# A two-layer macaron block on one core: the second feed-forward's first group moved into the slot attention's last two rounds, and the order at two other stage changes rewritten

## What is computed

```python
x = x + 0.5 * moe(ln(x))        # 8 experts, top 2, hidden = relu(x w1)^2
x = x + linear_attention(ln(x))
x = x + 0.5 * moe(ln(x))
x = x + 0.5 * ffn(ln(x))        # below
x = x + slot_attention(ln(x))   # 16 heads, softmax over the 8 batches of a position
x = x + 0.5 * ffn(ln(x))

def fp4_linear(x, w):           # both operands put on the FP4 grid in blocks of 16
    return fp4_quant_dequant(x) @ fp4_quant_dequant(w).T
h = silu(fp4_linear(x, w_gate)) * fp4_linear(x, w_up)   # 128 -> 352
y = fp4_linear(h, w_down)                               # 352 -> 128
```

## Time and profile before

| | us |
|---|---|
| median of 3 runs | 785.92 (783.46 to 788.07) |
| the profiled execution | 783.95 |
| its span, first to last instruction | 782.2 |
| busy: PE / DVE / ACT / POOL | 674.8 (86%) / 612.6 (78%) / 455.9 (58%) / 277.0 (35%) |
| mean granted TensorE clock | 0.95 |
| chain of waits: PE / DVE / ACT | 62% / 18% / 12% |

### The profile page before, as it was taken

How to read it: one execution, slowest core, us unless ns; L and a number is a source line. 1 busy time by engine, 2 the same in 40 slices (tenths; PEclk the granted TensorE clock), 3 DMA queues, 4 the chain that set the end, 5 groups by cost and what they waited for, 6 DMA issues and landing times.

```text
span 782.2 us, 16363 instructions
## 1 busy us (share of the span) xinstructions
PE 674.8 (86%) x5826; PEld 481.0 (61%) x5826; DVE 612.6 (78%) x1566; ACT 455.9 (58%) x863; POOL 277.0 (35%) x405
## 2 busy tenths in 40 slices
PE   4999999699999699999976999588888882799985
PEld 2777767568878667777743656355645651365654
DVE  2788778656675687788788999587999985699984
ACT  3777788647556067777864766356454215366752
POOL 5001120264554201001105686331543452367620
PEclk9999999789999899999998999889999996799998
DMA  8000000000000000000000000000000000000000
GB/s 208 12 0 0 0 1 1 2 3 4 2 0 4 2 1 1 0 0 0 1 2 0 1 0 1 1 0 1 2 0 0 0 1 0 0 14 28 13 28 28
DMA packets 13460, 7.08 MB, mean 9 GB/s; under 512 B 1176, under 2 KB 13408, under 8 KB 13408
## 3 DMA queue, kind: packets, MB, share of 16 engines
q1 hardware_dynamic: 11328, 5.33, 2.6%
q10 hardware_dynamic: 2080, 1.05, 0.5%
HBM read 4.28 MB, written 2.10 MB: 8 GB/s over the span
## 4 chain that ended last, share of the span: by engine, by line
PE 62%; DVE 18%; ACT 12%; issue 5%; POOL 2%; DMA 1%; DVEq 0%; ACTq 0%; POOLq 0%
PE ps L1390 57%; DVE shared L1226 3%; DVE shared L1198 3%; ACT ffn_work L509 2%; PE ps L1739 2%; ACT ffn_work L777 2%; PE ps L1398 1%; ACT xn L547 1%; DVE x_sb L1027 1%; ACT x_sb L785 1%; ACT ffn_work L770 1%; ACT xnT L554 1%; DVE stats L940 1%; DVE h_max L1301 1%; ACT hqT L781 1%
## 5 line engine op out<-in xcount | busy, mean ns | idle before, releaser
L1390 PEld LDWEIGHTS ps<-w_sb,sq_h 128*128 128x128 f32 x1024 | 131.7, 192 | 74.5 <-ACT sq_h L569 56.1
L1027 DVE SCALAR_TENSOR_TENSOR x_sb<-ps,gates,x_sb 128x128 f32 (+1 forms) x512 | 147.2, 344 | 24.7 <-PE ps L1390 21.0
L1390 PE MATMUL ps<-w_sb,sq_h 128*128 128x128 f32 x1024 | 138.0, 278 | 5.5 <-ACT sq_h L569 5.4
L1390 PE MATMUL ps<-xnT,w_sb 128*128 128x512 f32 x256 | 135.4, 613 | 0.0
L565 ACT ACTIVATE relu_h<-ps 128x512 f32<-128x512 f32 x128 | 75.6, 591 | 56.4 <-PE ps L1390 55.9
L353 POOL TENSOR_SCALAR vareps<-meanvar 128x4 f32<-128x4 f32 (+1 forms) x28 | 7.8, 278 | 276.2 <-DVE meanvar L949 275.7
L569 ACT ACTIVATE sq_h<-relu_h 128x512 f32<-128x512 f32 x128 | 80.6, 630 | 4.0
L1390 PE MATMUL ps<-gateT,xnT 128*128 128x352 f32 x128 | 59.5, 550 | 25.6 <-ACT ffn_work L777 21.9
L547 ACT ACTIVATE xn<-x_sb,shift,rstd 128x128 f32 (+1 forms) x136 | 56.9, 480 | 10.7 <-POOL shift L361 8.2
L1390 PE MATMUL ps<-downT,hqT 128*128 128x128 f32 x384 | 57.3, 288 | 4.3 <-ACT hqT L781 4.0
L400 POOL TENSOR_TENSOR shared<-shared 128x128 f32<-128x128 f32 x112 | 51.0, 455 | 27.7 <-ACT shared L646 19.5
(11 more groups left out here) (169 smaller groups left out, 1339.8 us busy)
## 6 DMA issues: line engine op xcount, KB each, us to landing
x_sb<-in_L_attn_x_dram SPq DMA_DIRECT2D x8, 256.0 KB, 7.4
out_dram<-x_sb SPq DMA_DIRECT2D x8, 256.0 KB, 2.3
w_sb<-in_L_ffn_w_all_dram ACTq DMA_DIRECT2D x2, 512.0 KB, 6.5
wraw<-in_L_attn_qkv_w_dram SPq DMA_DIRECT2D x1, 192.0 KB, 4.4
wraw<-attn_in_proj_weight_dram SPq DMA_DIRECT2D x1, 192.0 KB, 3.4
fraw<-in_L_ffn_w_down_dram SPq DMA_DIRECT2D x1, 176.0 KB, 2.9
fraw<-in_L_ffn_w_gate_dram SPq DMA_DIRECT2D x1, 128.0 KB, 2.8
fraw<-in_L_ffn_w_up_dram SPq DMA_DIRECT2D x1, 128.0 KB, 2.4
```

Of the source, the lines that this page charges most:

```text
L1027: t = nc.vector.scalar_tensor_tensor(tile_b(i, j), bank(4 + e % 4, TPB, C)[:, j, :], gates[:, j, e:e + 1], tile_b(i, j), ALU.mult, ALU.add)
L1390: return nc.tensor.matmul(o, a, b, start=start, stop=stop, **kw)
```

## The change

Six parts:

1. The FP4 step of x has one form for all groups: DVE `x_scales` (largest, scales, reciprocal) and one addition `x_snap`; POOL divides, subtracts and rescales; ACT `x_squares` and `x_offsets`. x always lies in the first half of `xn`, its quantised form in the second.
2. `moe_b` to `ffn_a`: ACT normalises half of the first x in the group before the last; DVE takes the scales at the start of the last group, ahead of the gates; `x_snap(0)` stands behind the third expert. In `ffn_a`'s group 0, `x_snap(1)` stands behind the product of the halves.
3. `ffn_a` to `att`: POOL does `x_back(7)` ahead of the attention's layer norm. TensorE transposes the attention's x and makes q and k before `x_under(7)`, v right behind it. ACT evacuates the transposed x before it writes group 6 out, takes v with q and k, and normalises the second slot's x inside group 7, half of it between the hidden transposes and half ahead of the last output.
4. In `att`, round 3 of 4: DVE takes the statistics of `ffn_b`'s group 0, POOL its layer norm ahead of the pairs, ACT normalises it.
5. In round 4: DVE `x_scales(0)`, statistics of group 1, `x_snap(0)`; POOL `x_divide(0)`, `layer_norm(1)` and `x_back(0)` between the pairs; TensorE the transposes of x into bank 2 and the four gate and up products between the contexts, with the gate through bank 6; ACT the silus. The Silu table load moves with them.
6. `ffn_b` then starts at the product of the halves of group 0, waits slot by slot for the attention's output, and does `x_scales(1)` and the third statistics ahead of that product.

Core of the diff:

```diff
                 def x_back(self, g):
                     pool.wait_ge(s["x_snapped"], g + 1)
+                    self.ch.link(nc.gpsimd.tensor_tensor(fq_x[0], fq_x[1], fq_x[0], ALU.subtract))
...
+                    for g in range(GROUPS):
+                        if g > 0:
+                            self.h_late(g - 1)
+                        if g + 1 < GROUPS:
+                            self.x_back(g + 1)
+                        if first and g >= GROUPS - 2:
+                            ln_group(S["att"], g - GROUPS + 2, B)
+                        if g + 2 < GROUPS:
+                            self.x_divide(g + 2)
...
                         slot_pairs(s, i)
+                    ffn_b.layer_norm(0)
                     slot_pairs(s, TPB - 2)
-                    slot_pairs(s, TPB - 1)
+                    ffn_b.x_divide(0)
+                    slot_pairs(s, TPB - 1, 0, 2)
+                    ffn_b.layer_norm(1)
+                    slot_pairs(s, TPB - 1, 2, 4)
+                    ffn_b.x_back(0)
+                    slot_pairs(s, TPB - 1, 4, B)
...
+                def last_body(i):
+                    scores_half(i, 0)
+                    exp_half(i, 0)
+                    scores_half(i, 1)
+                    x_squares(nxt, 0)
+                    x_offsets(nxt, 0)
+                    exp_half(i, 1)
+                    normal(nxt, False, 1)
+                    ctx_half(i, 0)
+                    x_out(i, 0)
+                    evac_xnT(nxt, 0, k=2)
+                    for j in range(TPB):
+                        silu(nxt, 0, j, 6)
+                    ctx_half(i, 1)
+                    x_squares(nxt, 1)
+                    x_offsets(nxt, 1)
+                    x_out(i, 1)
...
+            def normal(s, first, g):
+                act.wait_ge(s["rstd_ready"], g + 1)
+                if g > 0:
+                    act.wait_ge(s["x_divided"], g)
...
+                    if first and g == GROUPS - 1:
+                        front.xnT_half(0, 0)
+                        front.xnT_half(0, 1)
                     if g > 0:
                         x_out(g - 1)
                     if first and g == GROUPS - 1:
-                        front.xnT_half(0, 0)
-                        front.xnT_half(0, 1)
                         act.wait_ge(s_par, 64)
                         front.take_qk(0)
+                        front.take_v(0)
...
+            def x_scales(s, ch, g):
                 dve.wait_ge(s["xn_ready"], g + 1)
...
                 x4.nudged_scales()
-                x4.inverse(x4.sl)
-                x4.divide()
+                x4.inverse_out(s["x_inverse"])
+            def x_snap(s, g):
+                dve.wait_ge(s["x_sized"], 2 * g + 2)
+                nc.vector.tensor_tensor(fq_x[0], fq_x[1], fq_x[0], ALU.add).then_inc(s["x_snapped"], 1)
...
+                    if not first and not more:
+                        x_scales(nxt, ch, 0)
                     gating_end(i)
...
-                            if e == 1:
-                                x4 = x_head(nxt, ch, 0)
+                            if e == 0:
+                                ln_stats(nxt, ch, 1, TPB, tile_n)
                             if e == 2:
-                                ln_stats(nxt, ch, 1, TPB, tile_n)
-                            if e == 4:
-                                x_tail(x4)
+                                x_snap(nxt, 0)
...
+                    elif more:
+                        dve.wait_ge(s["xn_ready"], TPB)
+                        dve.wait_ge(s["out_free"], 3)
+                        ln_stats(nxt, ch, 0, TPB, tile_fb)
+                    else:
+                        x_scales(nxt, nxt_ch, 0)
...
+                    if not more:
+                        dve.wait_ge(s["out_free"], 4)
+                        ln_stats(nxt, ch, 1, TPB, tile_fb)
                     pv(i, 2)
                     pv(i, 3)
+                    if not more:
+                        x_snap(nxt, 0)
...
                     project_out(i, 0)
+                    if not more:
+                        pe.wait_ge(front.s["lin_ready"], 6 * TPB)
+                        x_transposes(nxt, 0, 2)
                     for b in range(4, B):
                         context(i, b)
+                        if not more:
+                            if b >= 6:
+                                pe.wait_ge(s["pv_ready"], B * i + 4 * (b - 5))
+                            gate_up(nxt, 0, b - 4, 6)
                     project_out(i, 1)
```

298 lines of the change are left out of this document (140 added, 158 removed).

## The result

| us | before | after |
|---|---|---|
| median of 4 runs each | 787.0 (783.46 to 788.85) | 758.67 (757.29 to 760.05) |
| profiled execution | 783.95 | 757.82 |
| span, first to last instruction | 782.2 | 756.0 |
| busy PE / DVE / ACT / POOL | 674.8 / 612.6 / 455.9 / 277.0 | 673.3 / 606.9 / 458.5 / 294.7 |

A forecast was written before the change was run, and what follows sets the result against it. Idle seams were taken as the loss, with stages full and VectorE setting 12.70 us per steady group. Gains 1.0 + 12.2 + 15.1 = 28.3 us, taken from the profiled 783.95, gave 755.6 us, range 750.5 to 765.

The forecast's parts named there:

- seam 1: Mixture of experts to first feed-forward: 1.0 us gained, bounds 0 and 2.6.
- seam 3: Slot attention to second feed-forward: 15.1 us gained, bounds 8 and 16.2.
- seam 2: First feed-forward to slot attention: 8.9 us from GpSimd's last x plus 3.3 from the attention's front; bounds 10 and 15.
- the new one about 7.2: First feed-forward's start: the changed kernel needs about 7.2 us from accumulations to first hidden product, where the first kernel needs 6.05.
- rival (b): End of first feed-forward: the last group's output slips by 3 us; gain 22 us, time 762, chance 0.10.
- A context 2.6: Attention's last round: gate and up pairs alternate with three contexts through one bank, 2.6 us from gate to gate.
- context 5 ends at 645.4: Attention's last round: the fifth context takes 1.2 us after x is evacuated at 644.9, ending at 645.4.
- Steady stretch at 0: Steady groups of the feed-forwards: nothing added, cost 0, covered by VectorE's full 12.70 us.
- Rival (d): Steady groups: GpSimd's slower layer norm adds 3.1 us to each of 14; time 799, chance 0.03.
- (e): Attention stretches by what is put in, second feed-forward starts where it did; gain 13 us, time 771, chance 0.04.
- Rival (a): Attention's interleaved last round is slow, TensorE pauses and falls to the lower clock; gain 21 us, time 763, chance 0.17.
- the drain: Table-load switches on the attention chain: about 1.38 us each by the Trainium skill, not added; with it 26.9 instead of 28.3.

The follow-up runs named there:

- order undone: Changed kernel with GpSimd again doing the attention's layer norm ahead of the last x near the end of the first feed-forward; 769.14 us.
- order alone: Kernel before the change with only GpSimd's last x put ahead of the attention's layer norm; 776.34 us against 784.44, ratio 0.9907.
- old front: Changed kernel with the front of the attention in its old order, GpSimd's new order kept; 761.07 us.
- yardstick: The changed kernel measured again, unedited, for comparison with the follow-up runs; 759.18 us.

## Why the prediction was right, and where it was not

The forecast of 28.3 us stands against 28.3 in the medians of the first measurement and 25.9 in those of the second; by the profiled executions, on which the sum was built, 26.1 came. That the medians of the first measurement give the forecast to the decimal is luck. The miss of 2.1 to 2.2 is almost one term: seam 1 is 2.2 off, seam 3 0.3 and the end 0.55, against 0.1 more in seam 2 and 0.85 from the stages ahead, whose code nobody changed.

- **Seam 1, predicted 1.0 (bounds 0 and 2.6), measured -1.2.** The step that failed: "the new one about 7.2, since ScalarE's silu of the second tile stands behind the squares of the second x, which now wait for GpSimd's divide". The mechanism was right and everything ahead of it (accumulations 2.6 earlier predicted, 3.1 measured); the size was not. The way from the accumulations to H is 9.15 and not 7.2; before it was 6.05. Of the 3.1 more, 1.3 lie ahead of the third tile's gate product (4.48 from the accumulations to 410.05, before 3.18 to 412.71): that is the queue, since GpSimd's divide can't begin before VectorE's scales behind the last accumulation and the wait runs to 408.17, and the prediction had 1.15 for it. The other 1.8 lie in the two tiles' products behind it (4.67 to H, before 2.87), of which three ran at the lower level; for these the prediction has no term. Another 0.7 is the second distance, 14.74 for 13.52, where 0.5 was allowed; and the accumulations gave 0.5 more than predicted. No bound went below 0. In the other seven traces with this order the seam lost 0 to 1.0, so 1.0 was too high in all of them. Moving one silu gave back 2.3 to 3.5. The stretch before, columns as in the earlier trace rows:

```profile
409.00:416.00 7.00, 5.20 (x18) 2.54 (x16) 5.95 (x18) 2.35 (x6) 2.87 (x4) 1.00 0.00 1
```

And after:

```profile
409.46:415.00 5.54, 4.30 (x8) 2.25 (x8) 0.28 (x1) 2.12 (x7) 0.62 (x2) 0.69 0.00 0
```

- **Seam 2, predicted 8.9 + 3.3, measured 9.25 + 3.1.** The last distance of a feed-forward is 12.38 and not 12.70 where nothing holds it (12.37 in the second feed-forward before, 748.28 to 760.65); the sum went by 12.70. Confirmed from both sides: order undone 21.37, order alone 12.38, old front 27.90. The single points hold as well: products of q and k start 12.03 after H (predicted 12.0), the last output of the feed-forward 20.34 after it (20.3; rival (b), the slip, did not happen), the reduction at 24.49 (24.3).
- **Seam 3, predicted 15.1, measured 14.8** (42.90 less 26.42, less 0.8 for the longer rounds, less 0.9 for the second distance). Right in sum, from two errors that cancel, and that is luck. "A context 2.6" a step was too long: 2.08, since the silu (636.53 to 636.99) is done while TensorE does the up product and the context, and adds nothing. And "context 5 ends at 645.4", 17.3 behind the sum, was too early: the first gate stands 18.8 behind it, since projection, transposes and context came one behind the other on TensorE without a shown wait (631.59 to 635.73), the projection at the lower level (2.08 for 1.16) and the transposes too (1.06 for 0.60). By the traces at the other level the seam would have gained 1.3 to 1.6 more. And the expectation that I drew from it, that the interleaving inside the last round carries nearly all of this seam, was wrong: 8.6 of the 16.5 come without it. (645.4 + 7.9 + 1.5 is 654.8 and not 654.9; nothing hangs on it.)
- **Steady stretch at 0:** held, 12.70 throughout, with GpSimd's layer norm at 5 us beside the passes (652.37 to 657.32). Rival (d) is out, and (e) too.
- **The end,** not in the sum: 0.55 longer, in code that the change leaves alone. The clock was 0.73 there and 0.84 before (761 to 782.2), but the yardstick's end took 22.09 at 0.82, so the clock alone doesn't explain it.
- **Rival (a)** in part: a stretch of the last round did run at 0.69 (625.5 to 633.5), ahead of the gates and not among them; they stood 2.08 apart.
- The table load: in the changed kernel it takes 1.28 at 635.17 and the first silu starts at 636.53 (before, 540.43 behind the load at 539.14); no drain as in the Trainium skill (ScalarE: Activation LUTs, What ACT_TABLE_LOAD costs) shows, as none did before. Leaving the drain out of the sum was right.

## What to carry to other kernels

Where a stage change leaves an engine idle, look first for one short instruction of a helper engine that stands behind work nobody awaits; here two swapped lines gave 8.1 of some 27 us. When work is pulled forward into such a gap, follow the queue of the engine that serves both sides: a bank emptied by an instruction queued behind somebody else's wait takes the gain back, and here TensorE's standing was followed by products at the lower level, 1.8 us more. Before crediting an edit with a shorter seam, look at which level the products ahead of it ran. And take the gain apart by experiments even where the total is right: of the seam that gained 16.5 us, half came without the interleaving, from steps made a round earlier and a shorter queue on ScalarE.
